# Seventy-two transposed blocks of a selective scan, scaled on ScalarE and summed on GpSimd instead of VectorE

## The chip, the cores and the metric

The kernel runs on one core of one Trainium2 chip. The metric is device time in microseconds of one execution. A core has five engines that run their own instruction streams in order and meet through semaphores: TensorE (PE; its weight loads are listed as PEld), VectorE (DVE), ScalarE (ACT), GpSimd (POOL) and SyncE (SP), which issues all DMAs here. PE writes to PSUM, eight banks of 128x512 float32.

## What is computed

One decoder layer over 4 sequences of 512 tokens, width 512: causal attention with rotary positions (16 heads of 32), a selective scan (Mamba style) over a context with its output gated by the layer's own stream, and a feed-forward block with ternary weights. Cut to what matters:

```
x = x + attention(layernorm(x)) @ w_o
# selective scan: 512 channels e, 16 states n, time l
u     = silu(conv(in_proj(ctx)) + conv_b)
delta = softplus(dt_proj @ dt_lo + dt_b);  A = -exp(A_log)
state[e,n] = state[e,n] * exp(delta[e] * A[e,n]) + (delta[e]*u[e]) * B[n]
y[e] = sum over n of state[e,n] * C[n]  +  D[e]*u[e]
x = x + (y * silu(layernorm(x))).T
x = x + ternary_ffn(layernorm(x))      # 512 -> 2048 -> gelu -> 512
```

The sum over n is where the change is.

## The kernel before

**The scan.** Channels lie on partitions, 4 groups of 128 channels (`ET`), time along the free dimension. For each sequence b and state n a "row" r is worked off in two pieces j of 2x512 elements: ACT writes the decay factors exp(delta*A) into PSUM banks 4 and 5 (kind `exp`, L1502), POOL writes delta*u*B into one of four buffers of `hb` (kind `dbu`, L1382, with B broadcast from DRAM into `b_bc`), DVE runs the recurrence over both (kind `scan`, L1911; L1919 in the last half-sequence). There is one set of factors for the full-length pieces, so the `exp` of a piece waits for the scan of the piece before. The last sequence is cut into two halves of time (L1919, `carry`). Ring `hb` holds two rows: the `dbu` of a row waits for the transposes of the row two before.

**The sum over states.** When both pieces of a row are done, PE transposes it, block of 128 times tb by block (kind `ht`, L1834: four 128x128 transposes into one PSUM bank, time on partitions), and DVE folds the bank into the sum: `y = bank * C[:, n] + y` (L1933, SCALAR_TENSOR_TENSOR of 128x512, C per partition from the tile `ct`). There are 256 such blocks: 16 states in 4 blocks over 4 sequences. The first addend of each sequence, D*u, is copied to `y_acc` by ACT (L1536).

**Beside it** run, for the same or the next sequence, attention (scores `s` with their row maxima on DVE, L2004 and L2008; exponentials `e` on ACT, L1615; transposes `t` on PE, L1808, copied by ACT, L1631; `pv`, `wo` with their readers on DVE), the projections (`rot`, `v`: L1765, L1778), softplus (`dt` on ACT, `delta` on POOL, L1395 to L1401), the rotary sums on POOL (L1416, L1417, L1423), and the ternary weights (`wsum`, `tern`). The feed-forward block of 16 token tiles (`fc`, L1881; `proj`, L1891; gelu on ACT, L1679; splits into two halves of precision on POOL, L1137) starts when attention of the last sequence is over, since its weights and buffers take the place of attention's.

**What sets the order.** `schedule()` gives every item a tick from tables of numbers; `follows()` lists, for each item, the engines it takes, a cost and what must come before; `plan()` builds each engine's fixed queue from them by list scheduling, chooses PSUM banks, and puts a few transposes of the identity on PE (`FILLS`, L1708) where it expects PE to stand still. Nothing is decided at run time: an instruction that waits holds up all behind it on its engine.

## Time and profile before

| | |
|---|---|
| three runs, median (lowest to highest) | 970.09 us (966.22 to 970.52) |
| the profiled execution | 970.87 us, of which the span is 969.1 us |
| mean granted TensorE clock | 0.979 |
| busy PE / DVE / ACT / POOL | 893.0 / 854.3 / 735.0 / 615.8 us |

Busy times are unions over an engine's instructions. PE is pipelined, so its busy share holds some of its own waiting for weights. Stages matter more than the whole: the first 100 us load and start, up to about 693 us attention and three of the four scans run side by side, and from there the feed-forward block runs beside the rest of the last scan. In the rows, "A <- B" is an instruction of A that stood idle until B released it.

### The profile page before, as it was taken

How to read it: one execution, taken by the hardware profiler on the slowest of the kernel's cores; microseconds unless marked ns; L12 is line 12 of the kernel's file. 1: busy time of each engine (PE TensorE's matmuls, PEld its weight loads, DVE VectorE, ACT ScalarE, POOL GpSimd, SP SyncE). 2: the span in 40 equal slices, each digit the busy share in tenths (PEclk: the TensorE clock that was granted, in tenths of full speed). 3: DMA queues.
4: the chain of work that ended last, by engine and by line, in shares of the span. 5: the costliest groups of instructions: out<-in, count | busy, mean ns of one | idle time of the engine just before them, and what ended most of it. 6: DMA issues, size and time to landing. Idle time of an engine off the chain costs nothing.

```text
span 969.1 us, 17249 instructions
## 1 busy us (share of the span) xinstructions
PE 893.0 (92%) x5426; PEld 573.7 (59%) x5426; DVE 854.3 (88%) x1167; ACT 735.0 (76%) x1476; POOL 615.8 (64%) x439
## 2 busy tenths in 40 slices
PE   7998779889999999989999999789889999999998
PEld 5464546556776656677656577567745455544544
DVE  4698999999999979899998989999989989998741
ACT  4988955935757996786988775896589999999551
POOL 0286954655347638993663989535679889878620
PEclk9999999799999999999999999799999999999999
DMA  6678849778847555274734645643147566755383
GB/s 211 234 225 267 224 124 230 197 206 216 225 144 205 165 182 148 72 210 112 185 101 136 206 132 183 220 110 111 38 72 179 112 135 129 151 106 125 62 166 77
DMA packets 146296, 153.55 MB, mean 158 GB/s; under 512 B 90448, under 2 KB 94800, under 8 KB 145952
## 3 DMA queue, kind: packets, MB, share of 16 engines
q1 hardware_dynamic: 146208, 152.45, 59.0%
q8 instruction: 46, 0.75, 0.3%
q14 instruction: 42, 0.34, 0.1%
HBM read 103.00 MB, written 28.44 MB: 136 GB/s over the span
## 4 chain that ended last, share of the span: by engine, by line
PE 45%; ACT 17%; DVE 15%; issue 11%; POOL 8%; DMA 3%; SPq 1%; ACTq 0%; POOLq 0%; DVEq 0%
PE ps L1765 7%; PE ps L1891 7%; PE ps L1834 6%; PE ps L1881 5%; DVE hb L1911 5%; ACT p_q L1615 4%; POOL hb L1382 4%; PE ps L1808 3%; ACT ps L1502 3%; PE ps L1778 3%; PE ps L1846 3%; DVE y_acc L1933 2%; ACT p_t L1631 2%; PE ps L1739 2%; DVE m_col L2008 2%
## 5 line engine op out<-in xcount | busy, mean ns | idle before, releaser
L1382 POOL TENSOR_TENSOR hb<-du,b_bc 128x1024 f32<-128x1024 f32 (+1 forms) x160 | 308.4, 1951 | 93.1 <-PE ps L1834 87.3
L1911 DVE TENSOR_TENSOR_SCAN hb<-ps,hb 128x1024 f32<-128x1024 f32 (+1 forms) x128 | 256.6, 2012 | 15.8 <-ACT ps L1502 12.2
L1502 ACT ACTIVATE ps<-delta,a_neg 128x511 f32<-128x511 f32 (+2 forms) x320 | 179.4, 598 | 86.2 <-DVE hb L1911 82.0
L1933 DVE SCALAR_TENSOR_TENSOR y_acc<-ps,ct,y_acc 128x512 f32<-128x512 f32 x256 | 178.6, 736 | 14.0 <-PE ps L1834 13.3
L1834 PE MATMUL ps<-ident,hb 128*128 128x128 f32 x1088 | 150.7, 281 | 24.8 <-DVE hb L1911 8.3
L1834 PEld LDWEIGHTS ps<-ident,hb 128*128 128x128 f32 x1088 | 124.0, 143 | 55.4 <-issue 16.5
L1615 ACT ACTIVATE p_q<-ps,m_col 128x512 f32<-128x512 f32 (+3 forms) x256 | 132.0, 538 | 10.5 <-DVE m_col L2008 9.5
L1765 PE MATMUL ps<-xn_t,w_ring 128*128 128x512 f32 x256 | 120.7, 616 | 1.0 <-ACT p_t L1631 0.5
L1881 PE MATMUL ps<-t_fc,xt 128*128 128x512 f16 x512 | 116.6, 379 | 1.8 <-ACT h_sb L1679 1.8
L1891 PE MATMUL ps<-t_pr,ht 128*128 128x512 f16 x512 | 113.0, 379 | 0.5 <-DMA ht<-hs 0.5
L1631 ACT ACTIVATE p_t<-ps 128x512 f32<-128x512 f32 x160 | 86.0, 612 | 26.8 <-PE ps L1808 26.6
L1808 PE MATMUL ps<-ident,p_q 128*128 128x128 f32 x640 | 88.0, 284 | 14.8 <-ACT p_q L1615 7.0
L1808 PEld LDWEIGHTS ps<-ident,p_q 128*128 128x128 f32 x640 | 73.0, 145 | 34.3 <-ACT p_q L1615 14.7
L2008 DVE TENSOR_REDUCE m_col<-ps 128x1 f32<-128x512 f32 (+2 forms) x192 | 86.3, 500 | 3.3 <-PE ps L1793 2.8
L1891 PEld LDWEIGHTS ps<-t_pr,ht 128*128 128x128 f16 x512 | 49.8, 98 | 60.2 <-issue 0.8
L1881 PEld LDWEIGHTS ps<-t_fc,xt 128*128 128x128 f16 x512 | 49.9, 98 | 55.0 <-ACT h_sb L1679 2.3
L1765 PEld LDWEIGHTS ps<-xn_t,w_ring 128*128 128x128 f32 x256 | 48.2, 198 | 53.7 <-issue 50.4
L1789 PE MATMUL ps<-k_st,q_st 128*128 128x512 f32 (+3 forms) x256 | 70.3, 377 | 7.8 <-DVE y_acc L1933 5.0
L1137 POOL TENSOR_TENSOR hs<-h_sb,hs 128x1024 f16<-128x1024 f32 x28 | 60.3, 2161 | 8.6 <-ACT hs L1669 8.6
L1416 POOL TENSOR_TENSOR hl<-hl 128x512 f32<-128x512 f32 x16 | 21.6, 1348 | 67.7 <-DVE hl L1996 67.7
L1778 PE MATMUL ps<-w_ring,xn_t 128*128 128x256 f32 x256 | 58.2, 381 | 2.5 <-DMA w_ring<-in_w_attn 2.2
L1846 PE MATMUL ps<-w_ring,o_t 128*128 128x256 f32 x256 | 57.4, 380 | 1.2 <-DVE xr L2031 1.0
(137 smaller groups left out, 1484.2 us busy)
## 6 DMA issues: line engine op xcount, KB each, us to landing
w_ring<-in_w_attn SPq DMA_DIRECT2D x32, 512.0 KB, 4.5
qk_d<-hl SPq DMA_DIRECT2D x64, 256.0 KB
q_st<-qk_d SPq DMA_DIRECT2D x64, 256.0 KB, 4.4
b_bc<-bc_d SPq DMA_DIRECT2D x48, 256.0 KB, 4.5
raw<-in_w_fc SPq DMA_DIRECT2D x16, 512.0 KB, 4.6
...
```

Of the source, the lines that this page charges most:

```text
L1382: nc.gpsimd.tensor_tensor(piece_of(e, hi, lo).rearrange("p (a n) -> p a n", a=2), du[b % 2][:, 2 * h:2 * h + 2, lo:hi], b_bc[:, i % BC_RIN ...
L1502: ins = nc.scalar.activation(factors(j, hi, lo)[:, (hi - lo) * m + start:(hi - lo) * (m + 1)], delta[b % 2][:, et, lo + start:hi], ACT.Exp ...
L1615: ins = nc.scalar.activation(p_q[:, h, Q_AT[i]:Q_AT[i] + w], src[:, col:col + w], ACT.Exp, bias=m_col[:, i, h:h + 1], accum_out=z_sum[:, b ...
L1631: nc.scalar.activation(dst, src, ACT.Copy).then_inc(p_ready, 1)
L1765: mm = nc.tensor.matmul(bank(kind, *a), w_ring[:, c % 2, d, P * half:P * half + P], xn_t[:, d, :], start=(d == 0), stop=(d == KD - 1))
L1808: mm = nc.tensor.transpose(dst[:, at:at + P], p_q[:, h, Q_AT[i] + P * jt:Q_AT[i] + P * jt + P], ident[:])
L1834: mm = nc.tensor.transpose(bank(kind, *a)[:, P * et:P * et + P], piece_of(2 * r + et // 2, hi, lo)[:, at:at + P], ident[:])
L1881: mm = nc.tensor.matmul(bank(kind, t, n), xt[:, t % 2, KD * m + d, :], t_fc[:, d, 512 * n:512 * n + 512], start=(d == 0 and m == 0), stop= ...
L1891: mm = nc.tensor.matmul(bank(kind, t), ht[t % 2][:, k // 8, 8 * m + k % 8, :], t_pr[:, k, :], start=(k == 0 and m == 0), stop=(k == FT - 1 ...
L1911: v.tensor_tensor_scan(h, d, h, 0.0, ALU.mult, ALU.add).then_inc(scan_done, 1)
L1933: v.scalar_tensor_tensor(out=y, in0=bank(kind, r, tb), scalar=ct[:, b % 2, tb, n:n + 1], in1=y, op0=ALU.mult, op1=ALU.add).then_inc(y_free ...
L2008: ins = v.tensor_reduce(m_col[:, i, h:h + 1], src[:, col:col + P * (i + 1)], AX.X, ALU.max, negate=True)
```

## The change

Of the sequences 0, 1 and 2, the blocks tb = 1 and 3 of the states from 1 to 10 (first sequence) or 1 to 13 (the other two) take another way: 20 + 26 + 26 = 72 blocks. ACT reads the PSUM bank and writes `bank * C` to a staging tile (the bank is free then), and POOL adds the staging tile to `y_acc`. Two staging tiles of 128x512 are used in turn; they lie in memory that another tile holds at other times: in the residual tile `xr[0]` for the first sequence, in `gate` for the other two. So there are new waits: the residual load of the first sequence waits for its 20 sums; the first staging of a sequence waits for the last reader of `gate` (and in the second sequence for the stores of the ternary weights, whose buffers share that memory); `gate` of the second half of the channels waits for the last sum of its sequence; ACT's scaling waits for the sum two before it, and a sum waits for the sum below it in the same block, whoever makes it. All tables of ticks and weights are replaced, so that every engine's queue stands in another order. The counts of all other items stay the same, except ACT's table loads (59 to 70 in the program, 36 to 45 of them behind the last `t`) and the identity transposes on PE (190 to 252).

```diff
+STAGED_TB, STAGED_TO = (1, 3), (10, 13, 13)
+STAGED = [[("ht", r, tb) for r in sorted(BEGUN) if ROWS[r][0] == b and 1 <= ROWS[r][1] <= STAGED_TO[b]
+           for tb in STAGED_TB] for b in range(B - 1)]
+STAGE = {item: n for staged in STAGED for n, item in enumerate(staged)}
+STAGE_SUM = {item: n + 1 for n, item in enumerate(x for staged in STAGED for x in staged)}
...
-WEIGHT = {'pe': {'ln1b': -40.55,
+WEIGHT = {'pe': {'ln1b': -60.08,
...
+def adder(item):
+    return "pool" if item in STAGE else y_reader(item)
...
-            [pe("pv", SLOTS // 2 - 1)] if b else [sp("xproj", 0)]
+            [pe("pv", SLOTS // 2 - 1)] if b else [sp("xproj", 0), pool(*STAGED[0][-1])]
...
-            yield "dve", 0.66, [pe(*item), (y_reader(before), before), act("ct", b)]
+            if item in STAGE:
+                n = STAGE[item]
+                yield "act", 0.5, [pe(*item), act("ct", b)] + ([pool(*STAGED[b][n - 2])] if n >= 2 else ...)
+                yield "pool", 1.27, [act(*item), (adder(before), before)]
+            else:
+                yield "dve", 0.66, [pe(*item), (adder(before), before), act("ct", b)]
...
+        def staging(item):
+            b = ROWS[item[1]][0]
+            return (gate if b else xr[0])[:, ET - 2 + STAGE[item] % 2, :]
...
 # SyncE, before the load of the residual
+                    if b == 0:
+                        sp.wait_ge(y_added, len(STAGED[0]))
...
 # GpSimd
+                elif kind == "ht":
+                    r, tb = a
+                    item = (kind, r, tb)
+                    y_taken(pool, item)
+                    y_summed(pool, (kind, row_before(r, tb), tb))
+                    y = y_acc[:, ROWS[r][0] % 2, tb, :]
+                    nc.gpsimd.tensor_tensor(y, y, staging(item), ALU.add).then_inc(y_added, 1)
...
 # ScalarE
+                    y_filled(act, item)
+                    if item in STAGE:
+                        emptied(act, TASK["ct", b])
+                        n = STAGE[item]
+                        if n >= 2:
+                            act.wait_ge(y_added, STAGE_SUM[item] - 2)
+                        elif b:
+                            y_filled(act, ("gt", b - 1, ET - 1))
+                            for k in range(2):
+                                act.wait_ge(t_stored[k], 16 * SUMS // 2)
+                        nc.scalar.activation(staging(item), bank(*item), ACT.Copy,
+                                             scale=ct[:, b % 2, tb, ROWS[r][1]:ROWS[r][1] + 1]).then_inc(y_free["act"], 1)
                         continue
...
+                    if 0 < b < B - 1 and et >= ET - 2:
+                        act.wait_ge(y_added, STAGE_SUM[STAGED[b][-1]])
...
 # VectorE
-                    if n is None:
+                    if n is None or (kind, *a) in STAGE:
                         continue
-                    y_taken(dve, (kind, row_before(r, tb), tb))
+                    y_summed(dve, (kind, row_before(r, tb), tb))
```

The two programs' queues are shown at one place, the middle of the second sequence's scan, on three engines. Line numbers of the changed kernel are some 32 to 54 higher: L1933 is L1987 there, L1911 is L1965, L1382 is L1415, L1502 is L1543; L1581 is the new scaling and L1491 the new addition. Here the scan is printed as a SCALAR_TENSOR_TENSOR that writes `hb`.

DVE from the scan of piece 44 on; `hb` is the recurrence, `y_acc` the sum over states, `m_col` the maxima of scores, `hl` the rotary products and `o_t` attention's output. Before:

```order
L1911 SCALAR_TENSOR_TENSOR hb<-ps,hb 128x1024
L2024 TENSOR_TENSOR o_t<-ps,rz_t 128x512
L1933 SCALAR_TENSOR_TENSOR y_acc<-ps,ct,y_acc 128x512
L1911 SCALAR_TENSOR_TENSOR hb<-ps,hb 128x1024
L1988 TENSOR_TENSOR hl<-ps,cos 128x512
L1989 TENSOR_TENSOR hl<-ps,sin 128x512
L1933 SCALAR_TENSOR_TENSOR y_acc<-ps,ct,y_acc 128x512 x6
L1911 SCALAR_TENSOR_TENSOR hb<-ps,hb 128x1024
L1995 TENSOR_TENSOR hl<-ps,sin 128x512
L1996 TENSOR_TENSOR hl<-ps,cos 128x512
L1911 SCALAR_TENSOR_TENSOR hb<-ps,hb 128x1024
```

And changed, from the scans of pieces 43 and 44 on:

```order
L1965 SCALAR_TENSOR_TENSOR hb<-ps,hb 128x1024 x2
L1987 SCALAR_TENSOR_TENSOR y_acc<-ps,ct,y_acc 128x512 x2
L1965 SCALAR_TENSOR_TENSOR hb<-ps,hb 128x1024
L2062 TENSOR_REDUCE m_col<-ps 128x1 x3
L1965 SCALAR_TENSOR_TENSOR hb<-ps,hb 128x1024
L1987 SCALAR_TENSOR_TENSOR y_acc<-ps,ct,y_acc 128x512
L2042 TENSOR_TENSOR hl<-ps,cos 128x512
L2043 TENSOR_TENSOR hl<-ps,sin 128x512
L1987 SCALAR_TENSOR_TENSOR y_acc<-ps,ct,y_acc 128x512
L2062 TENSOR_REDUCE m_col<-ps 128x1 x3
L1965 SCALAR_TENSOR_TENSOR hb<-ps,hb 128x1024
```

Between the same scans the folds went from one and six to two and two, and maxima of scores stand where folds stood.

POOL from the pieces 40 and 41 on; `hb<-du,b_bc` is `dbu`, `hl` the rotary sums, `delta` the softplus of the third sequence. Before:

```order
L1382 TENSOR_TENSOR hb<-du_96,b_bc 128x1024 x2
L1416 TENSOR_TENSOR hl<-hl 128x512
L1417 TENSOR_TENSOR hl<-hl 128x512
L1382 TENSOR_TENSOR hb<-du_96,b_bc 128x1024 x2
L1423 TENSOR_TENSOR hl<-hl 128x1024
L1395 TENSOR_SCALAR delta_99<-tmp 128x512
L1397 TENSOR_TENSOR delta_99<-tmp,delta_99 128x512
L1399 TENSOR_TENSOR delta_99<-delta_99,tmp 128x512
L1401 TENSOR_TENSOR delta_99<-delta_99,tmp 128x512
L1382 TENSOR_TENSOR hb<-du_96,b_bc 128x1024 x2
```

And changed:

```order
L1415 TENSOR_TENSOR hb<-du_96,b_bc 128x1024 x2
L1456 TENSOR_TENSOR hl<-hl 128x1024
L1491 TENSOR_TENSOR y_acc<-y_acc,gate 128x512 x2
L1415 TENSOR_TENSOR hb<-du_96,b_bc 128x1024 x2
L1491 TENSOR_TENSOR y_acc<-y_acc,gate 128x512 x2
L1415 TENSOR_TENSOR hb<-du_96,b_bc 128x1024 x2
L1491 TENSOR_TENSOR y_acc<-y_acc,gate 128x512
L1449 TENSOR_TENSOR hl<-hl 128x512
L1450 TENSOR_TENSOR hl<-hl 128x512
L1456 TENSOR_TENSOR hl<-hl 128x1024
L1415 TENSOR_TENSOR hb<-du_96,b_bc 128x1024 x2
```

The additions stand in ones and twos between the `dbu` of one row and of the next, and the four `delta` instructions have moved behind them.

ACT from the factors of piece 45 on (`a_neg`); `p_q` is attention's exponential, `p_t` its copy, `tmp` softplus, `gate<-ps,ct` the new scaling. Before:

```order
L1502 ACTIVATE ps<-delta_97,a_neg 128x511 x2
L1631 ACTIVATE p_t<-ps 128x512
L1502 ACTIVATE ps<-delta_97,a_neg 128x511 x2
L1631 ACTIVATE p_t<-ps 128x512
L1583 ACTIVATE tmp<-ps,small 128x512
L1584 ACTIVATE tmp<-ps,small 128x512
L1587 ACTIVATE tmp<-tmp 128x512
L1589 ACTIVATE tmp<-tmp 128x512
L1502 ACTIVATE ps<-delta_97,a_neg 128x511 x2
L1602 ACTIVATE v_109<-ps 128x512
L1502 ACTIVATE ps<-delta_97,a_neg 128x511 x2
```

And changed:

```order
L1581 ACTIVATE gate<-ps,ct 128x512 x2
L1543 ACTIVATE ps<-delta_97,a_neg 128x511 x2
L1654 ACTIVATE v_109<-ps 128x512
L1543 ACTIVATE ps<-delta_97,a_neg 128x511 x2
L1667 ACTIVATE p_q,z_sum<-ps,m_col 128x512
L1667 ACTIVATE p_q,z_sum<-ps,m_col 128x384
L1667 ACTIVATE p_q,z_sum<-ps,m_col 128x128
L1581 ACTIVATE gate<-ps,ct 128x512
L1683 ACTIVATE p_t<-ps 128x512 x2
L1683 ACTIVATE p_t<-ps 128x2x256
L1543 ACTIVATE ps<-delta_97,a_neg 128x511 x2
L1581 ACTIVATE gate<-ps,ct 128x512
```

The scalings stand between the factors of one piece and of the next, where the softplus of the third sequence stood.

## Rows read from the trace of the kernel before

**Rows 1.** The page's first part; columns busy us (share of span) xinstructions.

```profile
span 969.1 us, 17249 instructions
...
PE 893.0 (92%) x5426; PEld 573.7 (59%) x5426; DVE 854.3 (88%) x1167; ACT 735.0 (76%) x1476; POOL 615.8 (64%) x439
```

**Rows 2.** By stretch: us; PE, PEld, DVE, ACT, POOL busy us; clock, DMA, GB/s.

```profile
100.00:693.00 593.00, 542.34 (x3689) 381.68 (x3690) 558.70 (x737) 436.48 (x1011) 373.42 (x212) 0.97 0.58 164
693.00:969.10 276.10, 262.69 (x1376) 138.56 (x1374) 221.33 (x329) 223.15 (x348) 194.08 (x189) 1.00 0.57 117
100.00:150.00 50.00, 37.90 (x237) 25.10 (x238) 48.19 (x70) 37.83 (x97) 34.42 (x20) 0.91 0.62 166
550.00:600.00 50.00, 48.92 (x305) 39.36 (x304) 47.42 (x54) 36.88 (x80) 45.92 (x28) 1.00 0.54 163
```

**Rows 3.** Line L2031: duration ns min/median/max, first and last start us.

```profile
L2031 DVE TENSOR_TENSOR xr_last<-ps,xr_last x4: 666/674/691, 682.2 to 692.8; 128x512 f32<-128x512 f32 x4
```

**Rows 4.** Waits of PE, 100 to 693 us: us in total, times, longest.

```profile
PE ps L1834 <- ACT p_q L1615: 8.0, 7, 3.6
...
PE ps L1789 <- DVE y_acc L1933: 5.0, 4, 2.5
PE ps L1834 <- DVE y_acc L1933: 4.0, 3, 2.2
PE ps L1808 <- DVE y_acc L1933: 3.9, 3, 2.3
...
PE ps L1834 <- DVE hb L1911: 3.4, 4, 1.3
...
PE ps L1808 <- DVE y_acc L2055: 0.2, 1, 0.2
PE ps L1708 <- ACT p_q L1615: 0.2, 1, 0.2
```

**Rows 5.** Groups by shape: count, busy us, mean ns, idle before and its releaser.

```profile
L1382 POOL TENSOR_TENSOR hb<-du,b_bc 128x1024 f32<-128x1024 f32 x96 | 227.6, 2393 | 92.3 <-PE ps L1834 86.6 <-DMA b_bc<-bc_d 5.5
L1911 DVE TENSOR_TENSOR_SCAN hb<-ps,hb 128x1024 f32<-128x1024 f32 x96 | 218.8, 2280 | 9.7 <-ACT ps L1502 7.5 <-POOL hb L1382 1.7
L1933 DVE SCALAR_TENSOR_TENSOR y_acc<-ps,ct,y_acc 128x512 f32<-128x512 f32 x256 | 178.6, 736 | 14.0 <-PE ps L1834 13.3
...
L1631 ACT ACTIVATE p_t<-ps 128x512 f32<-128x512 f32 x160 | 86.0, 612 | 26.8 <-PE ps L1808 26.6
...
L1429 POOL TENSOR_TENSOR xr<-xr,y_acc 128x512 f32<-128x512 f32 x12 | 15.0, 1283 | 0.0
...
L1522 ACT ACTIVATE hb<-du,small 128x512 f32<-128x512 f32 x16 | 10.4, 717 | 6.1 <-PE ps L1834 6.1
...
L1536 ACT ACTIVATE y_acc<-ps 128x512 f32<-128x512 f32 x16 | 8.5, 599 | 1.3 <-PE ps L1834 1.1
```

**Rows 6.** Line L1933 alone, by stretch.

```profile
0.00:693.00 693.00, 130.48 (x188) 0.97 0.61 175
```

**Rows 7.** Waits of ACT, 100 to 693 us.

```profile
ACT ps L1502 <- DVE hb L1911: 80.3, 48, 5.1
```

**Rows 8.** Waits of DVE, 100 to 693 us.

```profile
DVE hb L1911 <- ACT ps L1502: 4.4, 7, 1.5
```

**Rows 9.** Waits of POOL, 100 to 693 us.

```profile
POOL hb L1382 <- PE ps L1834: 79.2, 24, 14.7
```

**Rows 10.** The chain that ended last, 685 to 800 us: start us, us, what.

```profile
745.68 1.28 ACT L1679
...
786.48 1.28 ACT L1679
```

**Rows 11.** Line L2079: duration ns min/median/max, first and last start us.

```profile
L2079 DVE TENSOR_SCALAR low<-raw,nthr x16: 729/744/2694, 121.2 to 289.3; 128x1024 bf16<-128x1024 f32 x16
```

**Rows 12.** The same view of line L1933.

```profile
L1933 DVE SCALAR_TENSOR_TENSOR y_acc<-ps,ct,y_acc x256: 653/740/752, 75.0 to 906.4; 128x512 f32<-128x512 f32 x128
```

**Rows 13.** Line L1708, the identity transposes, by stretch: PE and PEld busy us.

```profile
0.00:969.10 969.10, 28.71 (x190) 24.03 (x190) 0.98 0.59 158
```

More of the change, by code:

```diff
@@ L381 @@
-TILE = {'fxload': [67.7],
- 'xa': [-61.73],
- 'xc': [19.62],
- 'xt': [-153.78],
- 'fc': [63.84, -11.77, -60.85, 55.39],
- 'hstat': [-293.9],
- 'hn': [-257.45, -184.6],
- 'ht_ffn': [-10.09, 47.13],
- 'proj': [44.44]}
-FIRST_TILE = {'xa': [5.78], 'xc': [-2.03]}
-SWITCH = 42.4
+WEIGHT = {'pe': {'ln1b': -60.08,
+        'inproj': -76.97,
+        'xproj': 64.44,
+        'ct': -9.64,
+        'dt': 8.25,
+        'rot': -36.95,
+        'v': 11.57,
+        's': 2.88,
+        't': -14.65,
+        'pv': -64.26,
+        'rz': -42.62,
+        'wo': 28.62,
+        'ht': -5.07,
+        'gt': 108.45,
+        'wtot': 33.5,
+        'xt': 40.7,
+        'fc': -94.15,
+        'ht_ffn': 96.03,
+        'proj': 74.62},
+ 'act': {'carry': -65.06,
+         'exp': 32.6,
+         'skip': -106.33,
+         'ht': -101.08,
+         'ln1b': 225.77,
+         'inproj': -12.02,
+         'silu': 301.63,
+         'xproj': 154.55,
+         'ct': -233.5,
+         'dt': 49.29,
+         'hi': -91.36,
+         'v': -10.64,
+         'e': 159.56,
+         't': 141.27,
+         'pv': -80.95,
+         'rz': 1.9,
+         'gate': 78.5,
+         'xt': 46.74,
+         'ht_ffn': 22.81,
+         'fc': 18.39,
+         'wsum': 24.63,
+         'hn': -159.79},
+ 'dve': {'scan': 3.75,
+         'ht': 4.68,
+         'ln1a': 158.33,
+         'ln1b': 79.52,
+         'inproj': 33.51,
+         'delta': -79.89,
+         'rot': -99.7,
+         's': -5.23,
+         'rz': 27.84,
+         'pv': -184.22,
+         'wo': -34.56,
+         'ln2a': -1.13,
+         'ln2b': -166.51,
+         'gt': -107.0,
+         'wtot': 30.22,
+         'tern': -108.05,
+         'xa': 266.1,
+         'xc': -10.93,
+         'xt': 210.3,
+         'ht_ffn': 36.12,
+         'fc': -111.24,
+         'hstat': 290.3,
+         'hn': -171.05,
+         'hq': 38.82,
+         'proj': 219.83},
+ 'pool': {'delta': 2.48,
+          'dbu': 29.08,
+          'du': 22.49,
+          'lo': 132.21,
+          'xadd': -43.17,
+          'ln1a': -111.66,
+          'ln2a': 113.13,
+          'xa': -121.09,
+          'xc': -98.27,
+          'hstat': -122.02,
+          'rot': -158.56,
+          'xt': 49.62,
+          'ht_ffn': -48.16,
+          'ht': 38.82},
+ 'sp': {'xload': -143.43,
+        'cload': -25.9,
+        'wload': -136.77,
+        'lo': 9.85,
+        'xproj': -43.21,
+        'bcload': 51.62,
+        'stack': 180.72,
+        'resid': 148.0,
+        'x2store': -31.81,
+        'fwload': -131.45,
+        'fxload': -51.32,
+        'proj': 187.36,
+        'tstore': 132.14,
+        'twload': 61.98,
+        'xt': -102.33,
+        'ht_ffn': -47.58}}
@@ new lines @@
+LAST_STATE = {'exp': [90.38, 132.99],
+ 'dbu': [-107.22, -213.0],
+ 'scan': [-13.86, -183.82],
+ 'carry': [-45.94, -5.18],
+ 'ht': [-454.47, -34.04]}
+LAST_ROWS = [-314.78, -235.37, -76.2, -198.16, 127.62, -157.72, -231.91, -24.9, -85.92, -31.4, -9.51, 6.55, -212.62, 201.63,
+ -162.96, -72.16, -218.32, -28.66, -4.1, 74.14, -17.7, 78.92, -341.75, 86.17, -128.71, -87.09, 31.59, 95.66, 105.72,
+ 18.63, 13.97, -61.49]
+LAST_END = {'gate': [83.15, -66.11, -394.13, -17.27],
+ 'gt': [-454.81, -260.07, -182.04, -364.62, -345.29, 88.71, -403.19, -395.32],
+ 'xadd': [-576.18, -134.69, -167.17, -255.51]}
@@ L395 @@
+TILE = {'fxload': [160.15],
+ 'xa': [-194.32],
+ 'xc': [30.29],
+ 'xt': [-227.07],
+ 'fc': [17.42, -84.12, -70.46, -35.16],
+ 'hstat': [-404.88],
+ 'hn': [-181.12, -277.41],
+ 'ht_ffn': [20.83, -91.34],
+ 'proj': [71.43]}
+FIRST_TILE = {'xa': [-93.98], 'xc': [43.03]}
+SWITCH = 67.9
 PATIENCE = 0.18
@@ L505, in y_reader @@
 def y_reader(item):
-    return "act" if item[0] == "ht" and item[1] in SKIP_ROW else "dve"
+    return "act" if item[0] == "ht" and item[1] in SKIP_ROW or item in STAGE else "dve"
+def adder(item):
+    return "pool" if item in STAGE else y_reader(item)
 def follows(item):
@@ L1038, in layer_kernel @@
         y_free = {"act": sem("y_free_act"), "dve": sem("y_free_dve")}
+        y_added = sem("y_added")
         s_full = sem("s_full")
```

400 lines of the change are left out of this document (149 added, 251 removed), and 12 rows, old and new, of tables (ATTN_END, SKIP).

## The prediction

> **What bounds the kernel now.** I read the busy shares first, then busy time by stretch, then PE's waits in the stretch that the change touches, and the other engines' waits last.
>
> The shares alone name PE: 893.0 of 969.1 us busy, DVE next with 854.3 [rows 1]. By stretch it is not PE alone. Attention of the last sequence ends when the last `wo` block leaves at 692.8 us [rows 3]. From 100 to 693 us DVE is busy 558.70 of 593 us (94%), PE 542.34 (91%), ACT 436.48 (74%), POOL 373.42 (63%); behind 693 us PE leads with 262.69 of 276.1 us (95%) [rows 2]. The reader is to see two stages with two limits. In the first DVE is fullest and PE close behind it, and all but a few of the moved blocks lie there; the second is PE's, and the change moves little in it.
>
> What DVE costs in the first stage is read from PE, since PE's work has to be done anyway and its holes are the time to be won. PE stands idle 593 - 542.34 = 50.7 us there. Of its waits, eleven rows name a DVE instruction as the releaser, from 5.0 us down to 0.2 us, in sum 21.5 us; fifteen name ACT, from 8.0 us down to 0.2 us, in sum 25.8 us [rows 4]. Most of the first kind are PE waiting for a bank that a fold L1933 still has to empty.
>
> **The change, part by part.** *DVE loses 72 folds.* Before 693 us 188 folds keep DVE busy 130.48 us, 0.694 us each [rows 6] (the mean of 736 ns [rows 5] overlaps with neighbours). 72 x 0.694 = 50.0 us go, and DVE is left with 508.7 us. How much reaches the end is bounded by nothing on one side and, if the stretch kept DVE at its 94%, by 50.0 / 0.94 = 53 us on the other. I take neither, because PE has too little room: I take PE's idle time that DVE releases, **-21.5 us**. At 593 - 21.5 = 571.5 us DVE would be 89% busy and PE 95%, so PE would be next.
>
> *Clock.* The granted clock is 0.97 over this stretch, and 0.91 from 100 to 150 us, where PE was busy only 37.90 of 50 us [rows 2]; the two levels are 1.2 and 2.4 GHz. 0.03 x 593 = 18 us are lost to it at most. Fewer holes may win some back; I take a quarter, **-4 us**, with 0 and -18 as ends.
>
> *ACT gains 72 scalings.* No row has a copy out of PSUM with a scale per partition. The nearest are the plain copy from PSUM, 599 ns (L1536), and the scaled copy from SBUF, 717 ns (L1522) [rows 5]: 43 to 52 us, and I take 0.66 us, 47.5 us. ACT's load goes from 74% to (436.5 + 47.5) / 571.5 = 85%. What hides it: in 48 cases ACT stood ready before the scan and waited for it, 80.3 us in sum [rows 7], while DVE waited for the decay factors only 4.4 us [rows 8]. Not all is hidden, for behind a waiting scaling stand factors, exponentials and copies that PE wants. PE's 25.8 us of waits for ACT grow, and in proportion to ACT's load they become 30: **+4 us**. Ends: 0, and 47.5 us if every scaling stood in the way.
>
> *POOL gains 72 additions* of two SBUF tiles of 128x512, 1283 ns like L1429 [rows 5]: 92.4 us, POOL goes from 373.4 to 466 us, 82% of 571.5. It has the time: 79.2 us of it are waits of `dbu` for PE's transposes [rows 9]. By the queues, an addition stands behind the `dbu` pair that needs the same row's transposes, not ahead of it, so it holds up the next pair only when ACT is late. I count 0; the end is two additions ahead of each of the 36 staged rows' successors, 36 x 2.57 = 92 us, from which POOL's waits would have to be taken.
>
> *New waits.* The residual load of the first sequence now stands on SP until 20 additions are done, with broadcasts of B behind it; the last of the 20 stands in POOL's queue right behind the rotary item that SP's entry before this load waits for anyway. The waits for `gate` and the ternary stores lie likewise behind work that the queues put well ahead. 0, at most one broadcast's delay each.
>
> *The stage behind 693 us.* Nine more table loads stand on ACT there (36 to 45). Eight loads are on the chain that ended last between 740 and 790 us, 1.28 us each, the first and last of them at 745.68 and 786.48 us [rows 10]. 9 x 1.28 = 11.5 us is the upper end; 8 of 36 were on the chain, so 11.5 x 8/36 = **+2.5 us**. Nothing else in that stage changes its amount.
>
> *The port.* DVE's slowest SBUF-only instructions show what POOL can do to them: L2079 takes 744 ns as a rule and 2694 ns at worst [rows 11], while the fold, whose bank lies in PSUM, stays between 653 and 752 ns [rows 12]. The Trainium skill, "SBUF — State Buffer", section "Who interferes with whom", says that DVE with two SBUF inputs or in a two-port mode and a GpSimd instruction shut each other out for a whole instruction, while DVE with one SBUF input isn't touched. By that rule, with which both rows agree, the moved fold was free of POOL and its replacement isn't: if all 16 of L2079 met their worst, 16 x 1.95 = 31 us of the 50 would be given back, DVE's term would shrink to 21.5 x 19/50 = -8 us, and the sum would be 965 us. I keep the sum without it, as POOL stands in its own queue between them for most of the stretch.
>
> *Fillers.* 190 identity transposes cost PE 28.71 us [rows 13], 0.151 us each; 62 more are 9.4 us at most. They stand where PE waits, so 0.
>
> The sum against the profiled execution's own 970.87 us (span 969.1): 970.87 - 21.5 - 4 + 4 + 2.5 = 951.9, **19 us** less. The median shown is 970.09 us, 0.8 lower: 951 us.
>
> **The rivals.**
>
> *PE runs at its best rate.* From 550 to 600 us PE was busy 48.92 of 50 us, with DVE at 47.42 [rows 2]. If DVE's relief let PE hold 97.8% throughout, the first stage would last 542.34 / 0.978 = 554.5 us, 38.5 less, and with the tables' 2.5 the time is 970.1 - 36 = 934 us. For it: ACT's waits too are partly chains that start at DVE's maxima. Against it: PE never held that rate for 500 us, with three engines beside it at over 80%.
>
> *ACT takes the waits over.* DVE's 21.5 us and the clock's 4 go, but PE's waits for ACT double to 51.6 us: 970.1 - 25.5 + 25.8 + 2.5 = 973 us, about no change. For it: ACT's `p_q` is already PE's largest releaser [rows 4]. Against: ACT's 80.3 us of waiting [rows 7].
>
> *Slower: scalings stand in front of the decay factors.* The queues put one or two scalings between the factors of successive pieces; a scaling that waits for its transposes, or for the staging tile, holds the next factors, and with them the scan, whose set of factors is single. Price: the delay times 72, less 21.5 + 4 and plus 2.5. It decides from 23 / 72 = 0.32 us per scaling, half its own length. At 0.5 us: +36 - 23 = +13, 983 us. For it: scan and factors already alternate, 2280 ns for the scan [rows 5]. Against: DVE waited for factors 7 times only [rows 8].
>
> **How the numbers follow.** Forecast, 951 us: 0.50. PE at its best rate, 934 us: 0.20. ACT takes the waits over, 973 us: 0.13. Slower, 983 us: 0.17. A measurement of this kernel tells 0.5% (4.9 us) from no change. The first two make *faster* 0.70, the third *same* 0.13, the fourth *slower* 0.17. The forecast's own range is 940 to 964 us: its ends are the clock's whole 18 us and the port's bound. For 8 in 10 the range reaches from 931 us, below the best-rate case, to 974 us, over the case of no change, and leaves the slower one out.
>
> **What would show it.** Right: DVE busy falls by some 50 us and POOL rises by some 92, ACT by some 60; the last `wo` block leaves near 670 us; PE's waits for L1987 nearly vanish between 100 us and there, and those for ACT are below 35 us; the last stage lasts 276 to 280 us. Wrong: DVE's waits for factors or for `dbu` rise from a few us to some 25 or more, PE's idle time in the first stage stays near 50 us, or the last stage grows by more than 5 us.

## The result and the profile after

The changed kernel is slower: 988.45 us (median of 4 runs, 985.65 to 990.87) against 969.54 us for the kernel before, run beside it. The ratio is 1.0200, 95% interval 1.0163 to 1.0237. The forecast was 951 us; 988 lies outside its range, beyond even the slower rival.

The page of the changed kernel, first part; the profiled execution took 988.69 us. It answers to [rows 1].

```profile
span 986.8 us, 17521 instructions
...
PE 898.9 (91%) x5488; PEld 582.4 (59%) x5488; DVE 826.7 (84%) x1095; ACT 791.6 (80%) x1559; POOL 707.1 (72%) x511
```

The load moved as planned (ACT +56.6 us, POOL +91.3), but DVE lost only 27.6. The view by stretch, with the first stage now ending near 710 us (us; PE, PEld, DVE, ACT, POOL busy us; clock, DMA, GB/s), answers to [rows 2]; the row of `wo`'s last reader (duration min/median/max in ns, first and last start in us) to [rows 3].

```profile
100.00:710.00 610.00, 549.35 (x3750) 389.71 (x3751) 537.90 (x669) 484.99 (x1089) 465.81 (x284) 0.97 0.56 161
710.00:986.80 276.80, 263.56 (x1376) 139.16 (x1373) 214.35 (x328) 229.44 (x352) 191.26 (x187) 0.99 0.56 117
```

```profile
L2085 DVE TENSOR_TENSOR xr_last<-ps,xr_last x4: 661/682/692, 699.0 to 709.3; 128x512 f32<-128x512 f32 x4
```

Nearly all of the loss lies in the first stage. Its last `wo` block leaves at 709.3 us instead of 692.8, 16.5 us later, while from there to the end of the span it takes 277.5 us as against 276.3. From 100 to 710 us PE is idle for 610 - 549.35 = 60.7 us, 10 more than before in its first stage, and busy 7 us longer. Half of the delay is there early, when the last `wo` block of the first sequence leaves at 301.3 us instead of 293.3 (before, then changed):

```profile
L2031 DVE TENSOR_TENSOR xr<-ps,xr x4: 662/682/690, 274.1 to 293.3; 128x512 f32<-128x512 f32 x4
L2085 DVE TENSOR_TENSOR xr<-ps,xr x4: 659/684/693, 285.6 to 301.3; 128x512 f32<-128x512 f32 x4
```

PE's waits in that stage (us in total, times, longest), against [rows 4]:

```profile
PE ps L1862 <- ACT p_q L1667: 11.2, 22, 1.2
PE ps L1775 <- DVE x_in L2003: 6.1, 3, 4.1
PE ps L1843 <- ACT p_q L1667: 5.1, 2, 4.7
...
PE ps L1888 <- DVE hb L1965: 3.7, 4, 2.5
...
PE ps L1900 <- DVE y_acc L1987: 3.6, 1, 3.6
...
PE ps L1888 <- DVE y_acc L1987: 1.6, 2, 1.2
```

What the change aimed at did go: the rows that name `y_acc` sum to 5.2 us instead of 14.6. But all rows that name DVE still sum to 19.1 us (21.5 before), since layernorm's `x_in` and the scans came in, and those that name ACT rose from 25.8 to 41.3 us. Of these 15.5 us, 7.5 are for the exponentials `p_q`, and 6.3 for the new scalings (the rows with L1581), which PE never waited for before.

The waits of DVE, ACT and POOL in the same stretch, against [rows 8], [rows 7] and [rows 9]:

```profile
DVE hb L1965 <- ACT ps L1543: 22.7, 21, 2.8
DVE hb L1965 <- POOL hb L1415: 11.1, 6, 4.5
```

```profile
ACT ps L1543 <- DVE hb L1965: 57.2, 31, 4.8
...
ACT xr L1581 <- POOL y_acc L1491: 3.3, 2, 2.7
```

```profile
POOL hb L1415 <- PE ps L1888: 28.2, 9, 12.2
POOL y_acc L1491 <- ACT gate L1581: 24.3, 10, 5.4
```

DVE's scans now wait for factors 22.7 us (4.4 before) and for products 11.1 us. The rows show that they wait, and not who makes them wait; for the factors the experiments answer it otherwise than the rows suggest.

The groups by shape (count; busy us, mean ns; idle before and its releaser), against [rows 5]:

```profile
L1888 PE MATMUL ps<-ident,hb 128*128 128x128 f32 x1088 | 148.8, 279 | 26.8 <-DVE hb L1965 9.2 <-ACT p_q L1667 4.6 <-ACT v L1654 3.6
L1987 DVE SCALAR_TENSOR_TENSOR y_acc<-ps,ct,y_acc 128x512 f32<-128x512 f32 x184 | 130.8, 738 | 11.5 <-PE ps L1888 10.6
...
L1581 ACT ACTIVATE gate<-ps,ct 128x512 f32<-128x512 f32 x52 | 35.4, 695 | 5.5 <-PE ps L1888 5.3
L2135 DVE SCALAR_TENSOR_TENSOR tern<-raw,thr,low 128x1024 f16<-128x1024 f32 x16 | 31.4, 1960 | 0.6
...
L1491 POOL TENSOR_TENSOR y_acc<-y_acc,xr 128x512 f32<-128x512 f32 x20 | 27.4, 1380 | 14.3 <-ACT xr L1581 14.3
L2133 DVE TENSOR_SCALAR low<-raw,nthr 128x1024 bf16<-128x1024 f32 x16 | 22.9, 1434 | 0.0
L2003 DVE TENSOR_SCALAR x_in<-x_in,mv,rstd 128x512 f32<-128x512 f32 x16 | 20.7, 1311 | 0.9 <-POOL rstd L1468 0.9
```

The folds lost 178.6 - 130.8 = 47.8 us of DVE. Three kinds of DVE instructions, which read and write SBUF alone, took part of that back: `low` went from 1010 to 1434 ns in the mean, `tern` from 1712 to 1960, `x_in` from 696 to 1311, in sum some 20 us. Before they read:

```profile
L2081 DVE SCALAR_TENSOR_TENSOR tern<-raw,thr,low 128x1024 f16<-128x1024 f32 x16 | 27.4, 1712 | 0.6
L2079 DVE TENSOR_SCALAR low<-raw,nthr 128x1024 bf16<-128x1024 f32 x16 | 16.2, 1010 | 0.8 <-DMA t_d<-tern 0.8
L1949 DVE TENSOR_SCALAR x_in<-x_in,mv,rstd 128x512 f32<-128x512 f32 x16 | 11.1, 696 | 1.2 <-POOL rstd L1435 1.2
```

### The profile page after: what moved, and what is told of

Its sections match the earlier page's. It is cut to its first block, busy times and chain, and to the rows that moved or that the text cites. A ratio compares the mean times of both kernels' runs of the same rounds, so it can differ in the third digit from the quotient of the medians.

```text
span 986.8 us, 17521 instructions
## 1 busy us (share of the span) xinstructions
PE 898.9 (91%) x5488; PEld 582.4 (59%) x5488; DVE 826.7 (84%) x1095; ACT 791.6 (80%) x1559; POOL 707.1 (72%) x511
## 4 chain that ended last, share of the span: by engine, by line
PE 39%; ACT 26%; issue 14%; DVE 13%; POOL 7%; DMA 1%; ACTq 0%; SPq 0%; DVEq 0%; POOLq 0%
PE ps L1819 6%; ACT ps L1543 6%; PE ps L1945 5%; PE ps L1900 5%; PE ps L1888 4%; DVE hb L1965 4%; ACT p_q L1667 4%; PE ps L1935 4%; PE ps L1862 3%; POOL hb L1415 3%; PE ps L1832 2%; ACT L1524 2%; ACT h_sb L1733 2%; PE ps L1843 2%; ACT p_t L1683 2%
## 5 line engine op out<-in xcount | busy, mean ns | idle before, releaser
L1415 POOL TENSOR_TENSOR hb<-du,b_bc 128x1024 f32<-128x1024 f32 (+1 forms) x160 | 310.6, 1963 | 36.6 <-PE ps L1888 36.2
L1965 DVE TENSOR_TENSOR_SCAN hb<-ps,hb 128x1024 f32<-128x1024 f32 (+1 forms) x128 | 257.1, 2015 | 43.3 <-ACT ps L1543 29.9
L1543 ACT ACTIVATE ps<-delta,a_neg 128x511 f32<-128x511 f32 (+2 forms) x320 | 179.9, 601 | 63.1 <-DVE hb L1965 59.0
L1888 PE MATMUL ps<-ident,hb 128*128 128x128 f32 x1088 | 148.8, 279 | 26.8 <-DVE hb L1965 9.2
L1888 PEld LDWEIGHTS ps<-ident,hb 128*128 128x128 f32 x1088 | 123.0, 142 | 57.0 <-issue 18.8
L1987 DVE SCALAR_TENSOR_TENSOR y_acc<-ps,ct,y_acc 128x512 f32<-128x512 f32 x184 | 130.8, 738 | 11.5 <-PE ps L1888 10.6
L1819 PE MATMUL ps<-xn_t,w_ring 128*128 128x512 f32 x256 | 116.7, 598 | 1.9 <-ACT gate L1581 1.4
L1491 POOL TENSOR_TENSOR y_acc<-y_acc,gate 128x512 f32<-128x512 f32 x52 | 65.8, 1277 | 24.4 <-ACT gate L1581 24.3
L1843 PE MATMUL ps<-k_st,q_st 128*128 128x512 f32 (+3 forms) x256 | 73.5, 381 | 9.2 <-ACT p_q L1667 5.1
L1819 PEld LDWEIGHTS ps<-xn_t,w_ring 128*128 128x128 f32 x256 | 46.4, 190 | 53.1 <-issue 47.8
L1900 PE MATMUL ps<-w_ring,o_t 128*128 128x256 f32 x256 | 60.2, 393 | 3.6 <-DVE y_acc L1987 3.6
```

Of the source, the lines that this page charges most:

```text
L1415: nc.gpsimd.tensor_tensor(piece_of(e, hi, lo).rearrange("p (a n) -> p a n", a=2), du[b % 2][:, 2 * h:2 * h + 2, lo:hi], b_bc[:, i % BC_RIN ...
L1543: ins = nc.scalar.activation(factors(j, hi, lo)[:, (hi - lo) * m + start:(hi - lo) * (m + 1)], delta[b % 2][:, et, lo + start:hi], ACT.Exp ...
L1819: mm = nc.tensor.matmul(bank(kind, *a), w_ring[:, c % 2, d, P * half:P * half + P], xn_t[:, d, :], start=(d == 0), stop=(d == KD - 1))
L1888: mm = nc.tensor.transpose(bank(kind, *a)[:, P * et:P * et + P], piece_of(2 * r + et // 2, hi, lo)[:, at:at + P], ident[:])
L1900: mm = nc.tensor.matmul(bank(kind, *a)[:, CH * m:CH * m + CH], o_t[:, g, P * t:P * t + P], w_ring[:, wc % 2, g, :], start=(g == 0), stop=( ...
L1965: v.tensor_tensor_scan(h, d, h, 0.0, ALU.mult, ALU.add).then_inc(scan_done, 1)
```

## Experiments

Two theories stood at the start. *Work*: what ACT and POOL took over stands in the way there, and costs more than DVE's relief gives. *Relief*: DVE's 50 us were never worth 21.5 us, whoever takes the work. A rival to both was the new *orders* themselves. A cut instruction keeps its place, its waits and its signals, and works on 32 columns instead of 512. It is not gone: a cut fold still takes 242 ns in the mean, a cut addition 252, a cut scaling 289, so that what a cut shows is somewhat less than the whole price. A ratio is to the kernel before, run beside it, with its 95% interval; 0.1% is 1.0 us. Several results lie between the numbers that two theories had named, or beyond both; they are read as they stand.

### DVE's relief alone, in the old orders

The kernel before, with the same 72 folds cut:

```diff
-y = y_acc[:, b % 2, tb, :]
+w = 32 if (kind, r, tb) in STAGE else DM
+y = y_acc[:, b % 2, tb, 0:w]
```

> The kernel before, its queues untouched, with the same 72 folds on VectorE cut from 512 to 32 columns (the other 480 columns of these blocks are left out of the sum). It is the forecast's first step alone: VectorE is relieved and nobody takes the work. Theory A (VectorE's relief reaches the end, and what the change adds eats it): about 43 us of VectorE go and the time falls by some 20 us, to 945 to 955. Theory B (relief of VectorE is worth little, since ScalarE's factors and TensorE set the pace of the recurrence anyway): 963 to 970 us.

967.17 us, ratio 0.9965 (0.9944 to 0.9986): 3.4 us. The profiled execution took 971.0 us, the longest of its ten, so its waits are to be read for where they lie. By stretch, then PE's and DVE's waits from 100 to 693 us (line numbers are 4 or 5 higher than before):

```profile
100.00:693.00 593.00, 541.93 (x3690) 383.80 (x3691) 528.63 (x734) 435.93 (x1009) 372.12 (x212) 0.97 0.58 164
```

```profile
PE ps L1793 <- DVE y_acc L1938: 5.2, 3, 2.7
PE ps L1812 <- DVE y_acc L1938: 3.9, 3, 2.3
PE ps L1838 <- DVE y_acc L1938: 3.8, 3, 1.7
```

```profile
DVE y_acc L1938 <- PE ps L1838: 21.3, 20, 6.1
DVE hb L1915 <- ACT ps L1506: 8.9, 11, 2.0
DVE m_col L2013 <- PE ps L1797: 8.3, 10, 1.8
```

DVE lost 30 us of busy time in the stretch, and all of it became idle time: its folds wait for PE's transposes 21.3 us (12.9 before), and all of its rows that name PE sum to 43.9 us (21.3 before). PE's three largest rows for folds stand where they stood [rows 4]. The trace tells why. Ten waits of PE in the stretch end with a fold; nine of them end with one that was not cut, and in front of all ten DVE went from instruction to instruction without idle time. This is DVE (start us, us, what) before the longest, 2.7 us, which ends with the first of the last three folds:

```profile
209.44 0.24 DVE L1938 SCALAR_TENSOR_TENSOR y_acc<-ps,ct,y_acc 128x32 f32<-128x32 f32 x1
209.59 2.11 DVE L2084 TENSOR_SCALAR low<-raw,nthr 128x1024 bf16<-128x1024 f32 x1
211.74 3.26 DVE L2086 SCALAR_TENSOR_TENSOR tern<-raw,thr,low 128x1024 f16<-128x1024 f32 x1
214.92 2.28 DVE L1915 TENSOR_TENSOR_SCAN hb<-ps,hb 128x1024 f32<-128x1024 f32 x1
217.12 1.54 DVE L1938 SCALAR_TENSOR_TENSOR y_acc<-ps,ct,y_acc 128x512 f32<-128x512 f32 x3
```

So a fold releases its bank late by what stands ahead of it in DVE's queue (the ternary steps, a scan, maxima), and not because a fold is long. What the cut folds save is mostly spent in waiting for PE. Even here, where a cut fold lies ahead, the half microsecond that it saved is lost at once: this `low` took 1609 ns in the kernel before and 2.11 us now. The relief theory holds.

### The work taken over, cut

The changed kernel, POOL's additions and ACT's scalings cut, both and singly (the first two scalings stay whole):

```diff
-nc.gpsimd.tensor_tensor(y, y, staging(item), ALU.add).then_inc(y_added, 1)
+nc.gpsimd.tensor_tensor(y[:, 0:32], y[:, 0:32], staging(item)[:, 0:32], ALU.add).then_inc(y_added, 1)
...
-nc.scalar.activation(staging(item), bank(*item), ACT.Copy,
+w = DM if n < 2 else 32
+nc.scalar.activation(staging(item)[:, 0:w], bank(*item)[:, 0:w], ACT.Copy,
```

> The changed kernel, its queues untouched, with GpSimd's 72 additions cut to 32 columns and ScalarE's scalings too (but for the first two of each sequence): new orders, new waits and VectorE's relief stay, the work that the two engines took over is left out (480 columns of these blocks are not summed). Theory D (the work taken over): 945 to 960 us. Theory C (orders and waits): 975 us or more.

> The changed kernel, its queues untouched, with GpSimd's 72 additions alone cut to 32 columns (480 columns of these blocks are not summed). With both engines' new work cut the time was 972.0 us against 988.5 us, so 16 us are to be divided. Theory E (GpSimd: it shuts out VectorE's ternary and normalizing instructions and brings the products B*delta*u late): most of it goes, 972 to 977 us, and VectorE's L2133 is back near 1010 ns. Theory F (ScalarE: the scalings stand in front of factors and exponentials): little goes, 983 to 988 us.

> The changed kernel, its queues untouched, with ScalarE's scalings alone cut to 32 columns but for the first two of each sequence; GpSimd adds whole blocks (480 columns of what it adds are of an older block). Theory F: 972 to 977 us, and VectorE's waits for the decay factors fall from 22.7 us between 100 and 710 us to under 10. Theory E: 983 to 988 us, waits for the factors as before.

Both: 972.04 us, ratio 1.0014 (0.9997 to 1.0032). Additions alone: 979.0 us, 1.0115 (1.0077 to 1.0153). Scalings alone: 983.86 us, 1.0137 (1.0094 to 1.0181). So the work costs 1.0200 - 1.0014 = 1.9%, 18 us; the additions 0.85%, 8 us; the scalings 0.6%, 6 us. By the intervals the first is good to some 4 us, the second to 5 and the third to 6, so that the scalings' price is barely clear of noise. The work theory holds for the loss, and the relief theory again: with the work gone, 50 us off DVE and the new orders together come out at nothing.

Of the kernel with both cut, by stretch; PE's waits from 100 to 693 us; DVE's from 100 to 710 us; and groups by shape:

```profile
100.00:693.00 593.00, 541.68 (x3746) 387.77 (x3747) 528.80 (x668) 461.34 (x1088) 396.29 (x284) 0.97 0.58 165
```

```profile
PE ps L1863 <- ACT p_q L1668: 10.0, 18, 1.7
PE ps L1776 <- DVE x_in L2004: 8.8, 3, 5.4
...
PE ps L1889 <- DVE y_acc L1988: 1.4, 2, 0.9
```

```profile
DVE hb L1966 <- ACT ps L1543: 20.1, 19, 2.6
...
DVE hb L1966 <- POOL hb L1415: 4.5, 3, 2.8
```

```profile
L2004 DVE TENSOR_SCALAR x_in<-x_in,mv,rstd 128x512 f32<-128x512 f32 x16 | 19.6, 1241 | 0.9 <-POOL rstd L1468 0.9
L2134 DVE TENSOR_SCALAR low<-raw,nthr 128x1024 bf16<-128x1024 f32 x16 | 17.6, 1102 | 0.0
```

Most of the scans' waits for factors stay with scalings cut to a sixteenth of their columns, and so do most of the long `x_in` and PE's wait for it. These came with the new orders, not with the work. A cut scaling still waits for its transposes and its staging tile, but that is not it: ahead of none of these 19 waits does ACT stand idle before a scaling that lies between the factors and the ones before them. What stands there are attention's exponentials and copies and the softplus of the next sequence. The waits for products, and most of what `low` gained, are the additions' (4.5 us and 1102 ns here, 11.1 us and 1434 ns in the changed kernel). DVE's row for products, in the same stretch, with the scalings alone cut and with the additions alone cut:

```profile
DVE hb L1966 <- POOL hb L1415: 12.4, 6, 4.5
DVE hb L1965 <- POOL hb L1415: 5.9, 3, 3.4
```

The products are late mainly by the additions' own length. The first row alone would not show it, since POOL's additions still wait 30.2 us for scalings there (35.3 in the changed kernel); but with the additions cut they wait 60.4 us, and the products come earlier all the same. In the profiled executions the last `wo` block of the first sequence leaves at 295.6 us with the additions cut and at 294.1 with both. With both cut, PE's waits for folds sum to 2.6 us, those for ACT to 36.0: the new orders traded one for the other, with PE idle 51.3 us in all (50.7 before).

### Which additions: the first sequence's or the later ones'

```diff
+w = 32 if ROWS[r][0] == 0 else DM      # the second run: 32 if ROWS[r][0] else DM
```

> The changed kernel, with the 20 GpSimd additions of the first sequence alone cut from 512 columns to 32; the 52 others stay whole. Each theory starts from the cut of all 72, which took 9.5 us off. Port theory: DVE's instructions from SBUF to SBUF (the two ternary steps, 1434 and 1960 ns in the mean) lie in the first sequence, beside these 20 additions, so most of the 9.5 us belongs to them: 982.5 us, the two ternary steps back near 1200 and 1720 ns, the last wo block of the first sequence near 296 instead of 301 us. Late-product theory: 8.0 of the 11.1 us that DVE waited for POOL's products lie behind 300 us, beside the 52 other additions, so these 20 give little: 986 us, last wo of the first sequence near 300 us.

> The changed kernel, with the 52 GpSimd additions of the second and third sequences cut to 32 columns; the 20 of the first stay whole. Port theory: 985 us, the ternary steps stay at 1434 and 1960 ns, and the last wo block of the first sequence stays at 301 us. Late-product theory: 981 us, DVE's waits for POOL's products behind 300 us fall from 8.0 to about 5 us, and the stretch from the first sequence's last wo to the last sequence's shrinks from 408 to about 403 us.

985.31 us, ratio 1.0182 (1.0144 to 1.0219), and 985.61 us, 1.0177 (1.0144 to 1.0210): neither can be told from the changed kernel. In the first run, whose profiled execution took 992.92 us, the longest of its six, `low` and the last `wo` reader of the first sequence read (by shape, and by line within 200 to 370 us):

```profile
L2134 DVE TENSOR_SCALAR low<-raw,nthr 128x1024 bf16<-128x1024 f32 x16 | 19.9, 1243 | 0.0
```

```profile
L2086 DVE TENSOR_TENSOR xr<-ps,xr x4: 664/685/691, 284.9 to 300.3; 128x512 f32<-128x512 f32 x4
```

The instruction came back to 1243 ns, as the port theory said, and the block still left at 300.3 us (301.3 in the changed kernel). This does not clear the port. In this execution `x_in` rose to 1638 ns in the mean, so that `low`, `tern` and `x_in` sum to 74.7 us, as in the changed kernel (75.0); and from 150 to 200 us the granted clock was 0.83 instead of 0.90. In the second run DVE's waits for products behind 300 us fell from 8.0 to 5.9 us, and the ratio fell by 0.2%, which is within the noise. So cutting either half wins little that can be measured, and cutting all wins 8 us; which mechanism takes them stays open.

### Orders and staging apart

The kernel before with the new tables, and the changed kernel with the old tables:

```diff
-WEIGHT = {'pe': {'ln1b': -40.55,
+WEIGHT = {'pe': {'ln1b': -60.08,       # and all tables behind it; the reverse in the second run
```

> The kernel before with the changed kernel's tables of ticks and weights, and no block staged: the new orders alone, planned with folds on VectorE. Theory C (the new orders are what is slow): 980 us or more. Theories A and D (the staging's own work is what is slow, D: ScalarE's scalings in front of the decay factors and GpSimd's additions shutting out VectorE's two-input instructions): within 1% of 970 us.

> The changed kernel with the old tables of ticks and weights: 72 blocks staged, orders planned from the old ticks. Theory C (orders): back to 970 us or below, near 951. Theory D (the staging's own work): 980 us or more, with VectorE's waits for the decay factors over 20 us and the ternary line L2133 over 1300 ns where GpSimd's additions meet it.

1063.8 us, ratio 1.0969 (1.0942 to 1.0996), and 1036.75 us, 1.0686 (1.0655 to 1.0717). Both lie far above the 980 us that a theory had named as a lower end, and neither run separates anything: a table of ticks fits the set of items it was made for. They show what an order can be worth, 5 to 10%, against the 2% at stake.

### Relief of PE, of ACT, of all three

The kernel before: beside the cut folds, PE transposes one instead of four 128x128 blocks for each of the 72; then, with nothing else changed, 72 copies of `p_t` cut; then all three.

```diff
-for et in range(ET):
+for et in range(1 if ("ht", r, tb) in STAGE else ET):
...
+w = 32 if 8 <= p < 26 else 512      # the copy of p_t, source and destination
```

> The kernel before, its queues untouched, with the 72 folds cut to 32 columns as in the run of the folds alone (967.2 us), and of the 72 blocks' four transposes only the first made: TensorE is relieved of 216 transposes, 0.1385 us each by the group's 150.7 us for 1088, 30 us in sum. Theory G (TensorE sets the pace of the first stage, VectorE's 94% is a queue that waits with it): a good part of the 30 us reaches the end, 940 to 952 us. Rival H (the recurrence, scan and factors in turn, sets it): 962 to 967 us.

> The kernel before, its queues untouched, with 72 of ScalarE's 160 copies of transposed exponentials (L1631, slots 8 to 25) cut from 512 to 32 columns (what attention reads there is left from other slots): ScalarE is relieved by about 72 x 0.4 = 29 us, VectorE and TensorE not at all. Theory G, and ScalarE as TensorE's largest releaser in its waits (25.8 us): 955 to 965 us. Rival B (ScalarE has cover enough, 80 us of waits for the scan): 968 to 971 us.

> The kernel before, its queues untouched, with the three reliefs of the single runs at once: 72 folds cut to 32 columns, three of the four transposes of those blocks left out, and 72 of ScalarE's copies cut to 32 columns. Singly they gave -3.4 us (VectorE), nothing more (TensorE) and -1.9 us (ScalarE) against before. Theory I (the chain changes its engine every few us, so that a relief of one engine only makes it wait for another, and reliefs of several add up to more than their single gains): 945 to 960 us. Theory J (something else than these three sets the pace: the scan and its factors in turn, GpSimd or the clock): 962 to 967 us.

968.83 us, ratio 0.9998 (0.9978 to 1.0017); 966.8 us, 0.9979 (0.9960 to 0.9997); all three 961.43 us, 0.9909 (0.9874 to 0.9943). Of the first of them, by stretch:

```profile
100.00:689.00 589.00, 525.96 (x3485) 365.73 (x3486) 527.83 (x733) 434.65 (x1009) 371.48 (x211) 0.95 0.58 165
100.00:150.00 50.00, 38.63 (x224) 25.68 (x224) 44.83 (x67) 36.62 (x96) 32.58 (x19) 0.83 0.60 163
```

216 transposes less are some 30 us of PE (148.8 us for 1088 in the group L1888 above), and take only 15.5 us off its busy time (877.5 us in the program, 893.0 before [rows 1]), with the granted clock at 0.95 instead of 0.97 over the stage and at 0.83 instead of 0.91 from 100 to 150 us [rows 2]. What did leave the busy time became idle time: the end stands where it stood. PE's relief was only run beside the cut folds, and there it wins nothing more. Neither of these two runs, nor the cut folds alone, moves the end by more than 4 us; all three reliefs at once give 9, more than the 2 us of these two runs together.

### One turn of the loop, and its parts

Second sequence, kernel before: its 32 scans at half width, its 32 products at half width, then scans, products and factors together; and, for pairs 8 to 15, maxima, exponentials, transposes and copies of attention at half width.

```diff
+w = (1 if 2 * DS <= j < 4 * DS else 2) * (hi - lo)       # scan
+c = 1 if 2 * DS <= j < 4 * DS else 2                     # dbu
-for m in range(2):
+for m in range(1 if 2 * DS <= j < 4 * DS else 2):        # exp
...
-w = P * (i + 1)
+w = P * (i + 1) // (2 if 8 <= p < 16 else 1)             # attention, and so on
```

> The kernel before, its queues untouched, with the 32 scans of the second sequence run over half of their columns (the other channel group's recurrence is left out): 32 x (2.28 - 1.21) = 34 us less VectorE, as many as the cut folds, but on the turn of scan and factors. Theory K (that turn sets the pace): the time falls by 15 us or more, below 955 us. Theory I: by 3 to 8 us, as little as the folds' relief gave.

> The kernel before, its queues untouched, with the 32 products B*delta*u of the second sequence made for half of their columns (the other channel group scans what the buffer held): 32 x (2.39 - 1.29) = 35 us less GpSimd. If GpSimd's products set the pace of the scans: below 960 us. Theories I and K: within 4 us of before, as GpSimd waits 79 us for TensorE's transposes.

> The kernel before, its queues untouched, with scans, decay factors and products of the second sequence all made for half of their columns (one of two channel groups is left out): 34 us less VectorE, 21 us less ScalarE, 35 us less GpSimd, all on the turn of the recurrence within some 160 us. Theory K (that turn sets the pace): 945 us or less. Theory M (attention's chain sets it, the recurrence is fitted in between): 962 to 968 us, no more than the scans alone gave.

> The kernel before, its queues untouched, with attention of the second sequence (slots 8 to 15) made for half: maxima and exponentials over half of their columns, 12 of 20 transposes, copies of half the columns (what is left out stays from older slots). It is some 10 us less VectorE, 10 us less ScalarE in exponentials and 8 in copies, 9 us less TensorE, all on attention's chain. Theory M: 15 us or more, below 955 us, for as little as 10 us of any engine. Theory K: 965 us or more.

967.03 us, ratio 0.9974 (0.9957 to 0.9992); 968.97 us, 0.9992 (0.9976 to 1.0008); all of the recurrence 961.49 us, 0.9909 (0.9887 to 0.9931); attention 963.23 us, 0.9923 (0.9896 to 0.9950). The stretches of the second and third sequence in the kernel before, and that of the second with the recurrence halved:

```profile
293.00:447.00 154.00, 145.37 (x946) 99.85 (x945) 140.44 (x198) 122.60 (x271) 108.22 (x65) 1.00 0.59 166
447.00:605.00 158.00, 151.38 (x1012) 105.66 (x1014) 147.26 (x189) 122.84 (x274) 115.47 (x64) 0.99 0.51 147
```

```profile
292.00:440.00 148.00, 143.14 (x944) 99.82 (x941) 118.62 (x196) 111.19 (x250) 83.60 (x64) 1.00 0.59 171
```

This is the answer to what the middle stretches wait for. PE is busy 94% in the second sequence's (96% in the third's); with 22 us less on DVE, 11 on ACT and 25 on POOL it is busy 97%, and the stretch is 6 us shorter. PE's holes in it were 8.6 us in all, which bounds what relief of the other engines can win there while PE's own busy time stays. Neither theory's price came: the recurrence was to give 25 us if it set the pace and gave 9, attention 15 or more and gave 7.5, with less work for PE as well.

### Identity transposes

`FILL` at 1.0 in the kernel before (401 instead of 190 identity transposes), at 0.25 in the changed kernel (118 instead of 252) and in the one before (88):

```diff
-FILL, FILL_US = .5, 0.11
+FILL, FILL_US = .25, 0.11
```

> The kernel before with twice the identity transposes (the planner's share of an expected hole that it fills goes from 0.5 to 1), everything else in the same order. The granted clock was 0.97 from 100 to 693 us, up to 18 us. Theory L (the clock's dips cost time on the chain): the clock rises and the time falls by 3 to 8 us. Rival: TensorE is late by its fillers, the time is the same or 2 to 5 us longer.

> The changed kernel with half of its identity transposes (share of a hole that is filled 0.25 instead of 0.5; 252 fall to about half), same order otherwise. Theory N (fillers make TensorE late: they are some 4 us of the changed kernel's 19): 983 to 986 us. Rival: 988 us, or slower by a lower clock.

> The kernel before with half of its identity transposes, same order otherwise. Doubling them gave +6.6 us. Theory N: 2 to 4 us faster than before, 966 to 968 us. Rival: no change, or up to 5 us slower by a lower clock.

977.02 us, ratio 1.0068 (1.0046 to 1.0089); 992.76 us, 1.0218 (1.0179 to 1.0256); 968.33 us, 0.9976 (0.9955 to 0.9998). Identity transposes are not free: 211 more cost 6.6 us, at a mean clock of 0.977 that did not rise. But the 62 more of the changed kernel are not shown to be its loss: with 134 fewer it is no faster, at a clock of 0.964 instead of 0.981. The last is the one version that leaves nothing out and comes out below the kernel before, by 0.2%, too little to build on.

## Why the prediction was wrong

**The step that failed first** is the first term, "I take PE's idle time that DVE releases, -21.5 us". In the old orders, 30 us off DVE by cutting the same folds are worth 3.4 us; in the new ones, with the work cut too, relief and orders together are worth nothing. Two things were wrong in it. A wait of PE that ends with a fold was read as the price of the folds' length; it is the price of all that DVE does ahead of that fold, mostly ternary steps, scans and maxima, and what DVE was spared elsewhere it then waited for PE. And the room was taken over the whole stage, though half of it, the middle stretches, had PE at 94 to 96% already.

**The second** are the costs of the work. ACT's scalings were put at +4 us and measure 6 taken alone, within their bounds; POOL's additions were put at 0 and measure 8, within the bound of 92. Cut together they are 18 us; that this is more than the 14 of both lies within the noise. "It holds up the next pair only when ACT is late" was the reason for 0, and it fell: additions do wait for scalings (24.3 us in the row shown), but DVE's waits for products stay at 12.4 us when the scalings are cut and fall to 5.9 when the additions are, though these then wait longer for scalings.

**New orders** had no term of their own. They bring 16 us of new waits for factors and 8.5 us of longer `x_in` even with the work cut, and take away PE's waits for folds; net nothing. What they cost apart from the relief is open: by difference, if the relief is worth 3.4 us there too, about 5 us.

**The port.** `low`, `tern` and `x_in` rose by 20 us of DVE's time, of which some 12 came with the orders and 8 with the work (both cut: 17.6, 29.4 and 19.6 us). The Trainium skill, "SBUF — State Buffer", section "Who interferes with whom", has a DVE instruction in a two-port mode, or one with two SBUF inputs beside a GpSimd instruction that reads SBUF, contend with GpSimd's: whichever starts second is blocked until the first is done. The trace agrees for DVE, though no run shows the mode that it is in. Here a `low`, 0.73 us where it meets nothing, takes 2.94 and ends at 239.56 us, 0.55 us after a pair of POOL's products (start us, us, what):

```profile
236.62 2.94 DVE L2133 TENSOR_SCALAR low<-raw,nthr 128x1024 bf16<-128x1024 f32 x1
234.32 4.69 POOL L1415 TENSOR_TENSOR hb<-du,b_bc 128x1024 f32<-128x1024 f32 x2
```

Of the 14 `low` and `x_in` over 1.4 us in the changed kernel, 13 end so, 0.3 to 0.6 us behind an instruction of POOL that ran when they began, most often a product or a rotary sum and not an addition. Folds from PSUM kept their 738 ns. I kept the port's 31 us out of the sum. Whether it is a part of the loss is open: the run that was to bring the first sequence's part back did not lower DVE's sum.

**The clock** gave nothing (0.97 in both first stages; -4 forecast). **The last stage** grew by about 1 us (+2.5 forecast), with nine more table loads. **Fillers and new waits**, put at 0, are not shown to have cost the changed kernel anything, but that fillers stand only where PE waits is not so: 211 more cost the kernel before 6.6 us.

**The rivals.** "Scalings stand in front of the decay factors" had the sign, 983 us, and its mark, DVE's waits for factors up to 25 us, nearly came. Its mechanism is the smaller part of it: in the changed kernel scalings lie ahead of 11 of the 21 waits for factors, with lengths that explain 9.5 of the 22.7 us at most, and 16.4 us remain with the scalings cut, 20.1 with the additions cut as well. "ACT takes the waits over" is nearer: PE's waits for ACT did rise to 41.3 us, eating what the folds gave back, but 36.0 of them are there with the work cut too. PE's best rate came in places (49.82 of 50 us busy from 350 to 400 us, 47.41 before) and not over the stage (549.35 of 610 us).

In sum, against a forecast of -19 us: relief, orders and clock together +1, the work +18 (the last stage's 1 us is within these): +19.
